# VectorE chooses a node tile's experts behind the next tile's update instead of ahead of it (GNN layer and mixture of experts, one Trainium2 core)

## The reference, cut to what matters

```
x   = x + gnn(layernorm(x))      # edges, then for every node:
      r = sigmoid(i_r + h_r);  z = sigmoid(i_z + h_z);  n = tanh(i_n + r * h_n)
      h_new = (1 - z) * n + z * h;   bn = gamma * (h_new - mean) * rsqrt(var + eps) + beta
x   = x + ffn(layernorm(x))      # the second norm, then
      weights, selected = top_k(x @ Wg + bg, 2);  weights = softmax(weights)
      out = sum over the 2 experts of weight * (relu(x @ W1 + b1) @ W2 + b2)  +  0.5 * shared expert
```

## Time and profile before

| | |
|---|---|
| median of 3 runs | 1438.11 us (1437.27 to 1442.31) |
| the profiled execution | 1442.45 us, of which the span from the first to the last instruction is 1440.6 us |
| TensorE busy | 1378.2 us, 96% |
| VectorE busy | 1098.6 us, 76% |
| GpSimd busy | 900.3 us, 62% |
| ScalarE busy | 606.5 us, 42% |
| granted TensorE clock, mean | 0.989 |

### The profile page before, as it was taken

One profiled execution on the slowest core, in us unless ns is written; L12 is line 12 of the kernel. 1 busy time (PEld: TensorE's weight loads), 2 busy tenths in 40 slices (PEclk: granted clock), 3 DMA queues, 4 the chain that ended last, 5 costly groups with the idle time before them and its releaser, 6 DMA issues. The chain is left out here.

```text
span 1440.6 us, 22894 instructions
## 1 busy us (share of the span) xinstructions
PE 1378.2 (96%) x6714; PEld 1136.4 (79%) x6714; DVE 1098.6 (76%) x2746; ACT 606.5 (42%) x1088; POOL 900.3 (62%) x1037
## 2 busy tenths in 40 slices
PE   4899999999899999999999999999999999999996
PEld 3678888787678888888888888888888888888884
DVE  3586334234588988888888888888888888888885
ACT  3431212202244444445444544454445444544441
POOL 3210142102387788878887788778887788778871
PEclk9999999999999999999999999999999999999997
DMA  8211432246323223322332233223322332333220
GB/s 306 68 68 64 161 129 103 88 144 223 142 95 110 99 83 109 109 92 90 109 109 89 93 109 109 84 98 109 109 81 101 109 108 76 107 109 104 79 94 30
DMA packets 50625, 154.94 MB, mean 108 GB/s; under 512 B 7840, under 2 KB 8480, under 8 KB 50464
## 3 DMA queue, kind: packets, MB, share of 16 engines
q0 software_dynamic: 15920, 79.97, 16.3%
q1 hardware_dynamic: 34672, 74.55, 14.3%
HBM read 117.22 MB, written 37.28 MB: 107 GB/s over the span
## 5 line engine op out<-in xcount | busy, mean ns | idle before, releaser
L1455 PE MATMUL bank<-whh_hi,h_hi 128*128 128x512 f32 x948 | 384.4, 406 | 7.0 <-DVE h_lo L488 7.0
L1455 PE MATMUL bank<-whh_hi,h_lo 128*128 128x512 f32 x948 | 373.3, 394 | 0.0
L1455 PE MATMUL bank<-whh_lo,h_hi 128*128 128x512 f32 x948 | 371.3, 392 | 0.0
L1455 PEld LDWEIGHTS bank<-whh_hi,h_hi 128*128 128x128 f32 x948 | 178.6, 188 | 41.1 <-DVE h_lo L488 7.4
L1455 PEld LDWEIGHTS bank<-whh_hi,h_lo 128*128 128x128 f32 x948 | 178.1, 188 | 39.0
L1455 PEld LDWEIGHTS bank<-whh_lo,h_hi 128*128 128x128 f32 x948 | 179.0, 189 | 34.1
L1212 POOL DMA_INDIRECT gates<-gates_in,slot_at x79 | 119.1, 1507 | 64.7 <-POOL slot_at L1210 63.3
L1293 ACT ACTIVATE hn_raw<-bank 128x512 f32<-128x512 f32 x79 | 47.2, 597 | 259.9 <-PE bank L1455 259.9
L1251 POOL TENSOR_TENSOR h_n<-h,n_gate 128x512 f32<-128x512 f32 x79 | 102.5, 1297 | 58.7 <-ACT n_gate L1321 58.7
L1237 POOL TENSOR_TENSOR hn<-hn_raw,hn_bias 128x512 f32<-128x512 f32 x79 | 104.0, 1317 | 45.5 <-ACT hn_raw L1293 45.5
L1264 POOL TENSOR_TENSOR x_h_b<-x_h,bn_shift 128x512 f32<-128x512 f32 x79 | 103.4, 1309 | 20.9 <-ACT x_h L481 18.4
(11 more groups left out here) (176 smaller groups left out, 3179.3 us busy)
## 6 DMA issues: line engine op xcount, KB each, us to landing
xt<-in_x SPq DMA_DIRECT2D x79, 256.0 KB, 3.1
out<-y SPq DMA_DIRECT2D x79, 256.0 KB, 3.0
gates_in<-g_out SPq DMA_DIRECT2D x16, 768.0 KB, 3.3
wih_lo_raw<-in_wih_t SPq DMA_DIRECT2D x4, 768.0 KB, 16.1
whh_lo_raw<-in_whh_t SPq DMA_DIRECT2D x4, 768.0 KB, 7.6
gates_in<-late_out SPq DMA_DIRECT2D x6, 256.0 KB, 5.7
gates_in<-g_out SPq DMA_DIRECT2D x6, 256.0 KB, 2.0
m_lo_raw<-in_attr_t SPq DMA_DIRECT2D x5, 256.0 KB, 2.7
```

The lines of the kernel that those rows point to most:

```text
L1455: last = pe.matmul(to[0:R, :], a[:, s, k * R:(k + 1) * R], w[:, k, q * D:(q + 1) * D], start=n == 0, stop=n == 3 * DK - 1)
```

## The change

On VectorE the block that computes `f1`, `top`, `gap`, `top_i` and `top_f` of tile t-1 is written behind z's chain and the second norm's statistics of tile t, where it was ahead of them. No instruction is added or removed, and the waits in the block are the same. The other four engines' programs stay as they are, ScalarE's wait for `gap_done` included.

```diff
                     dve.tensor_tensor(z_pre[:, :], b_z[0:R, :], gates[:, s, D:2 * D], ALU.add).then_inc(z_pre_done, 1)
-                if p.has(-1):
-
-                    dve.wait_ge(f1_prod, t)
-                    dve.tensor_tensor(f1[:, :], b_f1[0:R, 0:F1], f1_bias[:, :], ALU.add).then_inc(f1_done, 1)
-                    dve.wait_ge(f1_done, t).then_inc(held["dve"], 1)
-                    dve.max(top[:, :], f1[:, 0:NE]).then_inc(top_done, 1)
-                    dve.wait_ge(top_done, t)
-                    wait_from(dve, weight_done, 2 * (t - 1))
-                    dve.tensor_tensor(gap[:, :], top[:, 0:1], top[:, 1:2], ALU.subtract).then_inc(gap_done, 1)
-
-                    dve.max_index(top_i[:, :], top[:, :], f1[:, 0:NE]).then_inc(top_i_done, 1)
-                    dve.wait_ge(top_i_done, t)
-                    dve.tensor_copy(top_f[:, :], top_i[:, 0:2]).then_inc(comb1_done, 1)
                 if p.has(0):
...
                     statistics(dve, p, 0, 2)
                     mean_var(dve, p, 0, 2)
+                if p.has(-1):
+
+                    dve.wait_ge(f1_prod, t)
+                    dve.tensor_tensor(f1[:, :], b_f1[0:R, 0:F1], f1_bias[:, :], ALU.add).then_inc(f1_done, 1)
+                    dve.wait_ge(f1_done, t).then_inc(held["dve"], 1)
+                    dve.max(top[:, :], f1[:, 0:NE]).then_inc(top_done, 1)
+                    dve.wait_ge(top_done, t)
+                    wait_from(dve, weight_done, 2 * (t - 1))
+                    dve.tensor_tensor(gap[:, :], top[:, 0:1], top[:, 1:2], ALU.subtract).then_inc(gap_done, 1)
+
+                    dve.max_index(top_i[:, :], top[:, :], f1[:, 0:NE]).then_inc(top_i_done, 1)
+                    dve.wait_ge(top_i_done, t)
+                    dve.tensor_copy(top_f[:, :], top_i[:, 0:2]).then_inc(comb1_done, 1)
```

## The result

The changed kernel takes 1628.08 us (median of 4 runs, 1626.77 to 1631.08), against 1438.4 us (4 runs) before: a ratio of 1.132, 95% interval 1.1295 to 1.1345. The forecast was 1620, range 1588 to 1660. The profiled execution has a span of 1625.5 us and a mean granted clock of 0.984.

What follows compares the result with a forecast made beforehand. TensorE bounds the kernel before at 13.14 us per period; the change closes a 15.5 us ring. 75 x 2.36 = 177, entry +4.2 and tail +0.5 give +182: 1624 profiled, 1620 us median, range 1588 to 1660.

Steps and rivals of the forecast that it cites:

- The links: Successive steps from the end of gap through ScalarE, GpSimd and VectorE to the next gap, claimed to add to 15.50 us.
- `x_h_b` to `shift`: On GpSimd, start of x_h_b to end of shift: taken as 2.20 us, between rows of 2.12 and 2.31.
- The entry: At h of tile 3, the first behind a late gap: a delay of 4.2 us, paid once.
- The link from ScalarE to GpSimd: End of ScalarE's x_h to start of GpSimd's x_h_b: taken as 0.10 us, bounds 0 and 0.2.
- Rival 1: VectorE's z_h_n waits for the end of GpSimd's rstd each period: 33 us more, 1653 us; chance 12%.
- the ring: Once-per-tile cycle of waits over ScalarE, GpSimd and VectorE, gap to gap: 15.5 us against 13.14; chance 79%.
- Rival 2: Only VectorE's own queue counts, ScalarE's wait being on no ring: period 13.70, 43 us more, 1481 us; chance 4%.
- The signs: Expected profile: h not waiting for one_rstd, weight waiting 4 to 5 us, TensorE waiting for h2, 84% busy, clock 1.00.
- Rival 3: z's chain starts 0.20 us sooner and TensorE's remaining waits go: at most 11 us faster, 1427 us; chance 1%.
- Rival 4: TensorE's clock falls after its pauses, half the matmul time at 1.2 GHz: 480 us more, about 1920 us; chance 3%.

Runs made afterwards that it cites:

- B: Changed kernel with ScalarE's weight sigmoids moved behind h and x_h of the next period: 1599.64 us, ratio 1.110.
- C: Kernel before with only top_i and top_f moved behind z's chain, f1, top and gap staying ahead: 1596.05 us, ratio 1.109.
- A with the filler: Kernel before with ScalarE's sigmoids waiting for the second norm's statistics, plus six discarded z gate matmuls per tile on TensorE: 1588.76 us.
- A: Kernel before, VectorE's order untouched, with ScalarE's weight sigmoids also waiting for the second norm's statistics of tile t: 1655.45 us, ratio 1.148.
- G: Changed kernel with GpSimd's x_h_b moved behind n_pre of the next period, nothing left out: 1546.26 us, ratio 1.075.

## Why the prediction was right

*Step by step.* The links by the two timelines, from the end of `gap`, forecast and measured: `h` +0.23, +0.24; end of `x_h` +1.75, +1.74; `x_h_b` +1.85, +1.83; end of `shift` +4.05, +3.94; end of `h_n` +10.29, +10.19; `z_h_n` 0.10, 0.10; `z_h_n` to `f1` 4.13, 4.11; to the end of `gap` 0.98, 0.98. Sum 15.50, 15.38. The one link that was mis-sized is `x_h_b` to `shift`: 2.11, the lower of the two rows, where I took a value between them. The entry was +4.2 forecast, and 410.23 - 405.92 = 4.3 measured. The link from ScalarE to GpSimd that no row of before showed took 0.09 us for my 0.10.

*Two things that I had not in the sum* brought it back to nearly the forecast mean: the ends of the loop (the mean of 15.36, 15.36, 15.45 and 15.70 is 15.47) and the clock (15.54 in all). From tile 3 to 78 that is 75 x 15.54 = 1165 us; I had 75 x 15.50. That 0.12 us too much in the links and 0.16 too little for these two nearly cancel is luck. Of the 8 us by which the median is above 1620, 3 are these periods. The other 5 come from the reference: the profiled execution of the kernel before was 4.3 us above its median, that of the changed kernel 0.8 below.

*The signs.* `h` no longer waits for `one_rstd`, TensorE waits for `h2` and is busy 86.0% from 600 to 1400 us (I had 84), VectorE waits 0.9 us ahead of `z_h_n`. `weight` waits 5.3 us for `gap`, a little over the 4 to 5 that I gave. One sign failed: the clock did not stay at 1.00.

*Rival 1* (VectorE and GpSimd hold each other up on the ring): `z_h_n` was not held by `rstd`; it starts 0.10 behind `h_n`, inside `rstd` in 77 of 79 tiles, and takes its usual 0.69 in all of them. `extra` was held in most periods, but off the ring, ahead of a wait for `h2`. Inside the changed kernel the rival is wrong. As soon as the ring is cut it is right, in another place and at a far higher price than my 33 us: B and C.

*Rival 2* (only VectorE's own queue, 13.70, 1481) is wrong, and worse than I said. It was worked out with VectorE's instructions at the durations of before, and B with the ring cut took 1600, 119 us more than this rival's sum. The forecast was right on the ring and would have been wrong on B. The changed order is slow for two reasons, each enough alone: the ring (A with the filler, 150 us above the kernel before) and what B and C show (158 to 161 us). They do not add: in the changed kernel VectorE waits for `h2`'s copies behind the held instructions anyway. How the second reason divides between the holds and the clock was not measured, since no filler was put into B or C. An upper bound for the clock there is the time that the mean clock took away: (1 - 0.954) x 1598 = 74 us in C against (1 - 0.989) x 1441 = 16 before, so at most some 58 us of 158; the same working gives 83 us for A, where 67 were measured.

*Rival 3* (faster): `z_h_n` came sooner relative to `h_n`, by 0.20, and TensorE gained nothing. I wrote there that `gap` comes about 4.8 us later; by the prediction's own links it is 0.10 + 4.13 + 0.98 = 5.21 behind `h_n` in place of 0.03, so 5.2.

*Rival 4* (the clock): I said that one pause of about 2 us should pass. Mostly it did; in five periods it did not, at a price of about 5 us, where I had 480 at 3%. The mechanism was real; the size was that of a few falls. In A it was 67 us.

*What stays open.* Why the clock falls in some periods and holds in others of the same pauses. That the holds start what makes B and C slow is read from their timelines; no run took the holds away with GpSimd's work left as it was. Why GpSimd's `rstd` does not hold up `z_h_n`: the prediction's guess, that it reads at once, was not tested.

## What to carry to other kernels

A block that is off the path of the busiest engine can still stand ahead of a wait on a third engine; ask what is queued behind the instruction that waits for the block's result, and follow it round until it either ends or comes back. If it comes back, the length of the ring can be added up from the rows: here to 1%, in the variants A and G to 2 or 3%, and in the changed kernel without `x_h_b` to 5%, in these three too short. But a rival that assumes that instructions keep their durations when they are moved is only as good as the alignment of VectorE and GpSimd: print what lies beside them in the new place.

## What the runs showed of the hardware

A few columns on VectorE (8 columns in `comb` and `extra`, 82 in the cast) can take 1.16 to 1.40 us instead of 0.17 to 0.28 when a GpSimd instruction of 128x512 runs, and in a row of three GpSimd instructions three of them in turn (C). One on 128x1 did not hold up `z_h_n`: 0.69 us in all 79 tiles of the changed kernel, in 77 of which it started while `rstd` ran.

TensorE's clock can fall to 1.2 GHz after pauses of 0.7 and 1.87 us with four transposes and six matmuls between them, and stay there for longer than the pause (until 1009 in the period shown). In A, where pauses of 1.9 to 2.0 us came every 15 to 16 us, the mean clock was 0.94. Matmuls with a discarded result in the pause gave back 67 us there.
